# Attention over 513 tokens: 128-row score tiles with the 513th token apart, two heads at a time in TensorE's row halves, and every other product in one PSUM bank

## The reference, cut to what matters

```python
b, l, _ = x.shape                      # 4, 513, 192; H = 8, DK = 64, DV = 24, N_POS = 32
h1 = _rmsnorm(x, norm1_w)
q = (h1 @ wq).reshape(b, l, H, DK)
k = (h1 @ wk).reshape(b, l, H, DK)
v = (h1 @ wv).reshape(b, l, H, DV)
basis = _rel_basis(l, N_POS)           # (513, 513, 32), depends on j - i alone
qw = jnp.einsum('bihd,hdn->bihn', q, w_pos)
qr = jnp.einsum('bihn,ijn->bhij', qw, basis)
uk = jnp.einsum('hd,bjhd->bhj', u_param, k)[:, :, None, :]
vw = jnp.einsum('hd,hdn->hn', v_param, w_pos)
vr = jnp.einsum('hn,ijn->hij', vw, basis)[None]
bias = (qr + uk + vr) * scale
scores = jnp.einsum('bihd,bjhd->bhij', q, k) * scale + bias
attn = jax.nn.softmax(scores, axis=-1)
out = jnp.einsum('bhij,bjhd->bihd', attn, v)
out = out.reshape(b, l, H * DV) @ wo + bo
x = out + skip
```

## Time and profile before

| | us |
|---|---|
| median of 3 runs | 1121.22 (1118.86 to 1128.76) |
| the profiled execution | 1127.92, its span 1126.0 |
| PE busy | 956.4 (85%) |
| DVE busy | 724.2 (64%) |
| ACT busy | 671.5 (60%) |
| POOL busy | 134.1 (12%) |

### The profile page before, as it was taken

One profiled execution on the slowest core, in us unless ns is written; L12 is line 12 of the kernel. 1 busy time (PEld: TensorE's weight loads), 2 busy tenths in 40 slices (PEclk: granted clock), 3 DMA queues, 4 the chain that ended last, 5 costly groups with the idle time before them and its releaser, 6 DMA issues. The chain is left out here.

```text
span 1126.0 us, 20694 instructions
## 1 busy us (share of the span) xinstructions
PE 956.4 (85%) x6722; PEld 825.2 (73%) x6722; DVE 724.2 (64%) x1567; ACT 671.5 (60%) x1196; POOL 134.1 (12%) x199
## 2 busy tenths in 40 slices
PE   2999999999978989897889888957869970999993
PEld 2999999999956766676567657736836650999992
DVE  6999979799437853876497449735653353555543
ACT  4656847668248864986597568844322314557555
POOL 1000000000001440244034304430000000000000
PEclk9999999999988998999999899987979995999996
DMA  7011101399326842683367238721001212422101
GB/s 238 20 55 30 52 10 33 65 134 142 60 68 188 274 120 63 209 262 104 113 219 240 58 113 253 233 72 37 1 1 29 56 28 72 112 65 72 45 0 56
DMA packets 78721, 112.67 MB, mean 100 GB/s; under 512 B 10917, under 2 KB 38866, under 8 KB 78562
## 3 DMA queue, kind: packets, MB, share of 16 engines
q1 hardware_dynamic: 78658, 111.93, 37.7%
HBM read 61.07 MB, written 47.68 MB: 97 GB/s over the span
## 5 line engine op out<-in xcount | busy, mean ns | idle before, releaser
L405 PE MATMUL psum<-w,feat 128*128 128x192 f32 x960 | 166.0, 328 | 0.0
L405 PEld LDWEIGHTS psum<-w,feat 128*128 128x128 f32 x960 | 155.4, 191 | 0.0
L792 POOL TENSOR_SCALAR a_scores<-a_scores,a_inv 112x514 f32<-112x514 f32 (+1 forms) x160 | 112.6, 705 | 299.9 <-DVE a_inv L1138 299.9
L1123 DVE CUSTOM_DVE_ANT_0 a_scores<-psum,a_bias 112x514 f32<-112x514 f32 (+1 forms) x160 | 109.7, 688 | 49.6 <-PE psum L865 41.1
L422 PE MATMUL psum<-w_parts,parts 128*128 128x384 f32 x384 | 120.2, 378 | 24.4 <-DVE parts L228 21.5
L1015 ACT ACTIVATE a_scores<-a_scores,a_least 112x514 f32<-112x514 f32 (+1 forms) x160 | 116.6, 729 | 14.1 <-DVE a_least L1123 13.5
L878 PE MATMUL psum<-ident,a_scores 112*112 112x112 f32 (+1 forms) x800 | 103.4, 262 | 14.0 <-DVE a_probsT L1133 8.8
L328 ACT ACTIVATE feat<-turn 128x1024 f32<-128x1024 f32 (+1 forms) x60 | 58.4, 974 | 86.0 <-DVE turn L211 47.3
L865 PE MATMUL psum<-a_kh,a_q 128*112 128x258 f32 (+1 forms) x320 | 100.1, 334 | 7.1 <-DVE a_q L1093 4.2
L878 PEld LDWEIGHTS psum<-ident,a_scores 112*112 112x112 f32 (+1 forms) x800 | 78.5, 138 | 36.6 <-POOL a_scores L792 16.9
L819 PE MATMUL psum<-h1T,place 96*128 (+3 forms) x320 | 87.8, 413 | 13.3 <-DVEq L1086 6.9
(11 more groups left out here) (217 smaller groups left out, 1777.0 us busy)
## 6 DMA issues: line engine op xcount, KB each, us to landing
shear<-a_pos SPq DMA_DIRECT2D x128, 224.9 KB, 3.8
a_bias<-shear SPq DMA_DIRECT2D x128, 224.4 KB, 3.9
shear<-zero SPq DMA_DIRECT2D x20, 448.9 KB, 17.8
e_fc<-in_e_fc_dram SPq DMA_DIRECT2D x8, 672.0 KB, 5.8
x<-in_xT_dram SPq DMA_DIRECT2D x20, 256.0 KB, 2.8
e_proj<-in_e_proj_dram SPq DMA_DIRECT2D x8, 576.0 KB, 6.4
shear<-a_pos SPq DMA_DIRECT2D x32, 130.5 KB
a_bias<-shear SPq DMA_DIRECT2D x32, 130.3 KB
```

The source lines that it names most:

```text
L405: mm = pe.matmul(sums[m][:, 0:D], feat[:, r, j, 0, 128 * m:128 * m + 128], w[:, k, :], start=False, stop=ends)
L792: pool.tensor_scalar(row, row, inv[0:TILES[g % NT][1], g % TT:g % TT + 1], 1.0, ALU.mult, ALU.mult).then_inc(weighed, 1)
L1123: dve.tensor_tensor_reduce(halves(scores[0:r, g % TT, 0:PADL]), psum2(score_pair(g), r), halves(bias[0:r, g % MR, :]), -1.0 / 8, BIG, ALU. ...
```

## The change: what it does

- A score tile has 128 queries, so a head has four tiles and an image 32. Query 513 of all eight heads is computed apart (`score_row`, `row_position`, `row_values`, in 36 partitions), and key 513 is left out of the transposes: its probabilities come through a small matmul (`last_keys`) and one more matmul in `values`. Tiles go in the order head within a group of four heads, tile, group.
- Two heads are scored together (`score`). Head 2p lies in partitions 0 to 63 of `q` and `k`, head 2p+1 in 64 to 127. Per window of 258 keys there are three terms (hi hi, lo hi, hi lo), each as two matmuls of 64 rows, one for each head, into banks of their own. One call fills banks 0 to 3 and waits until both tiles of the pair before have been read.
- `put` moves a tile's four blocks in one copy, ACT the even tiles and DVE the odd ones, from bank 6. `position` uses banks 4 and 5.
- Everything else is one of 41 jobs an image, all in bank 7. A job waits for `job_out` of the one before. An image has 16 steps of two tiles, with one to three jobs in a step: step 0 keys and q; 1 values and q; 2 two projects and k; 3 two projects and keys; 4 v, v and keys; 5 v_last, values and k; 6 q, q, keys; 7 k, k, row_position; 8 p, p, keys and the extra row; 9 values and q; 10 q, k, keys and the row's transpose; 11 row_values and k; 12 q, q, keys; 13 values and p; 14 p, k, keys; 15 k. A q, k or p job is one window of 257 columns for one pair of heads or group.
- Products of the next image (`OF_NEXT`, 12 jobs) and the end of the image before (`OF_BEFORE`, 6 jobs) stand among the tiles, so an image has no part without tiles. Image 0 is written out, images 1 and 2 loop, image 3 is written out, and `finish` ends it. Twelve products (`START`) come first.
- `stack` for the next image is split: 12 DMAs after step 9 and 12 after step 15 on SP. The second copy of keys (L994, L1104) is gone. The 97-row input copy `load_image` moves from DVE to POOL.

The diff, cut to its core:

```diff
+    ROWS, NTILE, PAIRS = s.SROWS, N // s.SROWS, H1 // 2
+    NG, NU2 = H1 * NTILE, H1 * NTILE // 2
+    AHEAD, LAG = 8, 4
+    RT, MR, TT, RING = 4, 8, 8, s.RING
...
+    TERMS = (("hi", "hi"), ("lo", "hi"), ("hi", "lo"))
...
+    head_of = lambda g: G4 * (g // (G4 * NTILE)) + g % G4
...
+    pair_of = lambda u: 2 * (u // (2 * NTILE)) + u % 2
...
+    JOBS = [
+        ("keys", 1, 3), ("q", 2, 0),
...
+        ("p", 0, 0), ("p", 0, 1), ("keys", 0, 3),
...
+    JOBS_AT = [2, 2, 3, 3, 3, 3, 3, 3, 3, 2, 3, 2, 3, 2, 3, 1]
...
+    OF_BEFORE = [n for n, (kind, a, i) in enumerate(JOBS) if kind == "project" or (kind, a, i) in (("keys", 1, 3), ("values", 1, 1))]
+    OF_NEXT = [n for n, (kind, a, i) in enumerate(JOBS) if (kind in "qk" and a < 2) or kind == "p"]
...
+            def image(b, first, more):
+                for u in range(NU2):
+                    for g in (2 * u + AHEAD, 2 * u + AHEAD + 1):
+                        if g < NG:
+                            store(b, g, first)
+                        elif more:
+                            store(b + 1, g - NG, False)
+                        if g - LAG < NG:
+                            load(b, g - LAG, first)
+                        elif more:
+                            load(b + 1, g - LAG - NG, False)
+                    if more and u == 9:
+                        stack(b + 1, 0)
+                    if more and u == NU2 - 1:
+                        stack(b + 1, 1)
 
             stack(0, 0)
...
+            def last_keys(b, hg, t):
+                g = hg * (NG // 2) + G4 * t
+                pe.wait_ge(weighed, b * NG + g + G4)
+                stand_alone(pe, passed)
+                return pe.matmul(s.bank[JOB][32 * hg:32 * hg + G4, 0:ROWS],
+                                 scores[:, g % TT:g % TT + G4, L - 1:L].rearrange("p g n -> p (g n)"), s.ident[:, :],
+                                 start=True, stop=True)
...
+                for jb in range(NTILE):
+                    for n in range(G4):
+                        h = hg * G4 + n
+                        pe.matmul(s.bank[JOB][VW * n:VW * n + VW, 0:2 * ROWS], v[:, jb, VW * h:VW * h + VW],
+                                  probsT[:, n, jb, 2 * ROWS * w:2 * ROWS * (w + 1)], start=jb == 0, stop=False, skip_group_check=True)
+                return pe.matmul(s.bank[JOB][:, 0:2 * ROWS], v_last[:, 128 * hg:128 * hg + 128],
+                                 lastT[:, 2 * ROWS * w:2 * ROWS * (w + 1)], start=False, stop=True,
+                                 skip_group_check=True)
...
+            def job(b, n, first, more):
+
+                kind, a, i = JOBS[n]
+                pe.wait_ge(job_out, NS + NJ * b + n)
+                if (first and n in OF_BEFORE) or (not more and n in OF_NEXT):
+                    pe.sem_inc(job_out, 1)
...
+            def score(b, u, first):
+                p, i0 = pair_of(u), ROWS * tile_of(2 * u)
+                if u or not first:
+                    pe.wait_ge(biased, b * NG + 2 * u)
+                if u == 9:
...
-                    for w in range(2):
-                        for k in (kh, kl):
-                            mm = pe.matmul(pairs[score_pair(g)][w][0:r, 0:HALF + 1], q[:, h, i0:i0 + r],
-                                           k[:, h, w * HALF:w * HALF + HALF + 1], start=k is kh, stop=k is kl)
...
+                for w in range(2):
+                    for n, (q_part, k_part) in enumerate(TERMS):
+                        for e in range(2):
+                            rows = slice(DK1 * e, DK1 * e + DK1)
+                            mm = pe.matmul(s.bank[2 * e + w][:, 0:HALF + 1], q[q_part][rows, p, i0:i0 + ROWS],
+                                           k[k_part][rows, p, w * HALF:w * HALF + HALF + 1], start=n == 0, stop=n == 2)
+                            if w == 1 and n == 2:
+                                mm.then_inc(scores_done, 1)
...
+            def score_row(b):
+                pe.wait_ge(biased, b * NG + 2 * 8 + 1)
+                pe.wait_ge(row_q_set, b * 2 + 2)
+                pe.wait_ge(job_out, ended(b, "k", 3, 1))
+                stand_alone(pe, passed)
+                for w in range(2):
+                    for p in range(PAIRS):
+                        for n, (q_part, k_part) in enumerate(TERMS):
+                            mm = pe.matmul(s.bank[w][0:RW, 0:HALF + 1], row_q[:, p, ("hi", "lo").index(q_part), :],
+                                           k[k_part][:, p, w * HALF:w * HALF + HALF + 1], start=p == n == 0, stop=p == PAIRS - 1 and n == 2)
...
+            def flip(b, g, first):
+                pe.wait_ge(weighed, b * NG + g + 1)
+                if g % 2:
+                    pe.wait_ge(put_a, b * (NG // 2) + g // 2 + 1)
+                elif g or not first:
+                    pe.wait_ge(put_d, b * (NG // 2) + g // 2)
+                for jb in range(NTILE):
+                    mm = pe.transpose(s.bank[FLIP][:, ROWS * jb:ROWS * jb + ROWS], scores[:, g % TT, ROWS * jb:ROWS * jb + ROWS],
+                                      s.ident[:, :])
...
+
+                score(b, u, first)
+                job(b, jobs[0], first, more)
+                behind(2 * u - 2)
+                ahead(2 * u + AHEAD)
+                if len(jobs) > 1:
+                    job(b, jobs[1], first, more)
+                ahead(2 * u + AHEAD + 1)
+                behind(2 * u - 1)
+                if u == 8:
+                    score_row(b)
+                if u == 10:
+                    pe.wait_ge(put_d, b * (NG // 2) + 10)
+                    flip_row(b)
+                if len(jobs) > 2:
...
+                act.wait_ge(job_done, count)
+                if kind == "p":
+                    if not first:
+                        act.wait_ge(stacked[a], 16 * 3 * G4 * i)
+                    act.copy(parts[:, a, 0, window(w)], s.bank[bank][:, 0:HALF]).then_inc(hi_done, 1)
+                    if w:
+                        act.wait_ge(rest1, i * 4 + a * 2 + 2)
+                        act.copy(parts[:, a, 1, :], rest[:, :]).then_inc(part2, 1)
+                else:
+                    if not first:
+                        last = 2 * NTILE * (a // 2) + 2 * NTILE - 2 + a % 2
+                        act.wait_ge(scores_done, i * NG - NG + 2 * last + 2)
+                        act.wait_ge(row_scored, i)
+                    dst = (q if kind == "q" else k)["hi"]
+                    act.copy(dst[:, a, window(w)], s.bank[bank][:, 0:HALF]).then_inc(hi_done, 1)
...
+                jobs = list(range(first_job(u), first_job(u) + JOBS_AT[u]))
+                job(b, jobs[0], first, more)
+                weigh(b, 2 * u)
+                if 2 * u + AHEAD < NG:
+                    position_out(b, 2 * u + AHEAD, first)
+                elif more:
+                    position_out(b + 1, 2 * u + AHEAD - NG, False)
+                if u:
+                    put(b, 2 * u - 2, first)
+                elif not first:
+                    put(b - 1, NG - 2, False)
+                if len(jobs) > 1:
+                    job(b, jobs[1], first, more)
+                weigh(b, 2 * u + 1)
+                if u == 8:
+                    weigh_row(b)
+                if u == 10:
+                    put_row(b)
+                if len(jobs) > 2:
+                    job(b, jobs[2], first, more)
+
...
-                    dve.wait_ge(rest1, i * 2 + p + 1)
-                    dve.sem_inc(prod_free, 1)
+                    dve.tensor_tensor(rest[:, window(w)], s.bank[bank][:, 0:HALF], parts[:, a, 0, window(w)], ALU.subtract).then_inc(rest1, 1)
+                    dve.wait_ge(rest1, i * 4 + a * 2 + w + 1)
+                    dve.sem_inc(job_out, 1)
                 else:
...
+            def add_bias_row(b, first):
+                dve.wait_ge(row_scored, b + 1)
+                dve.wait_ge(job_out, ended(b, "row_position", 0, 0))
+                if not first:
+                    dve.wait_ge(job_done, ended(b - 1, "row_values", 0, 0))
+                stand_alone(dve, passed)
+                dve.tensor_tensor_reduce(halves(row_scores[:, :]), psum2(0, RW), halves(row_bias[:, :]), -1.0 / 8, BIG, ALU.add,
+                                         ALU.min, row_least[:, :]).then_inc(row_biased, 1)
...
+                add_bias(b, 2 * u, first)
+                add_bias(b, 2 * u + 1, first)
+                job(b, jobs[0], first, more)
+                invert(b, 2 * u)
+                if len(jobs) > 1:
+                    job(b, jobs[1], first, more)
+                if 2 * u + AHEAD + 1 < NG:
+                    position_out(b, 2 * u + AHEAD + 1, first)
+                elif more:
+                    position_out(b + 1, 2 * u + AHEAD + 1 - NG, False)
+                if u:
+                    put(b, 2 * u - 1, first)
+                elif not first:
+                    put(b - 1, NG - 1, False)
+                invert(b, 2 * u + 1)
+                if u == 8:
+                    add_bias_row(b, first)
```

(4 more changed lines are left out.)

834 lines of the change are left out of this document (423 added, 411 removed), and 9 rows, old and new, of the table JOBS.

## The result

Slower. The changed kernel takes 1152.63 us in the median (1151.0 to 1155.27), against 1121.78 for the kernel before on the same chip: ratio 1.0261, 95% interval 1.0218 to 1.0305. The forecast was 1111. The profiled execution has a span of 1149.2, against 1126.0 before; all of these 23.2 us lie in the attention.

A forecast was written before the change was run, and what follows sets the result against it. Before, PE was busy 88% of each image with some 20 us of waits; after, a chain of ACT's and DVE's lists around one bank. Start -11, images 0, tail +1 gave 1118 profiled, 1111 median; range 1078 to 1152.

The forecast's parts named there:

- the sum: Whole kernel: start -11, images 0, tail +1, giving -10 against the profiled execution, 1118.
- Start: Before the first bias addition: it comes at about 341 instead of 352.3, a gain of 11 us.
- The chain: Inside the images: ACT's list, then DVE's, in series around one bank; plain step 5.5 us, looped image 100.
- No engine is full: Plain step of 5.5 us: PE's own work is 4.35 and DVE's 3.9, so no engine fills it.
- covered, with about 1 us to spare: SP after steps 9 and 15: loads behind 7.6 us of stack DMAs, issued 12 to 13 us ahead, arrive in time.
- Biases come late: Rival, chance 0.08: slower stack or loads behind it cost up to 5 us at six places; +30, 1141.
- PE waits for a DVE put: Step 10, before the 513th query's transpose: this wait is part of a step priced at 6.9 us.
- 34 one-column matmuls: Step 11, for the 513th query: they take 3 us (bounds 1 and 5) of a 7.1 us step.
- Tail: After the last addition: 14.5 us against 13.5, four projects through one bank; a loss of 1.
- Shape changes: Rival, chance 0.14: array shape changes cost PE up to 0.17 us, two in each of 64 steps; +22, 1133.
- the last two rivals: Row halves not running at once, chance 0.13, +42, 1153; biases coming late, chance 0.08, +30, 1141.
- The forecast of no gain in the images: Four images: 384 us against 383.7 before; product stages vanish and their work returns as longer steps.

The follow-up runs named there:

- e7_mute: Loads of stack spread, plus ScalarE's and VectorE's copies of sixteen query and key products an image dropped, against e1_spread; 1134.3 us, ratio 1.0086.
- e8_lighter: Against e1_spread, fewer TensorE matmuls for the value rows (4 for 8 a job) and the 513th query's scores (8 for 24); 1133.38 us.
- e6_one_half: Against e1_spread, both heads of a pair take queries and keys from rows 0 to 63; 1203.37 us, ratio 1.0662.
- e3_fill: Against the changed kernel, TensorE also runs unread products in the last image; 1145.24 us, ratio 1.0174.
- e9_flip_later: Against e5_best, the 513th query's flip moved behind step 11's scores and its values to step 11's second product; 1126.48 us, ratio 0.9992.
- e12_loads: Against e11_both, the four load groups for the next image's first half issued one place earlier each; 1119.43 us, ratio 0.9941.
- e11_both: Against e5_best, the edits of e9_flip_later plus the 513th query's scores made in the middle of step 8; 1122.88 us, ratio 0.9978.
- e2_serial: Against the changed kernel, three score matmuls of head 0 put ahead of head 1's, not alternating; 1153.87 us, ratio 1.0247.
- e4_noprod: Against the changed kernel, query and key products among the tiles left out, the first image's reused; 1148.94 us, ratio 1.0175.
- e5_best: Against the changed kernel: loads spread, last image filled, last four projections each in a bank of its own; 1136.38 us, ratio 1.0095.
- e1_spread: Against the changed kernel, each head's three stack DMAs issued at a step of their own; 1145.23 us, ratio 1.0165.

## Why the prediction was wrong

Against the profiled execution before, the sum said 10 us less and the profile has 23.2 more. The 33 us between them lie in the four images, 4.0, 6.9, 8.1 and 9.9, and in the tail, 3.6.

**Start: right.** The first bias addition stands at 341.2, forecast 341.

**The chain: right in kind.** The plain step is 5.5, step 8 is 9.1 (forecast 9.2), and the copies of the products are on the chain of the thin steps (e7_mute). But "No engine is full" holds of the plain step alone. In step 4 TensorE's own work sets the length (e8_lighter), where the forecast had it by way of ACT's exponential, and step 8 goes in part with TensorE's work. For steps 1, 5, 9 and 13 it is argued, not shown: with the loads spread, PE is busy for 96 to 100% of them in the third image. That every step grew in e6_one_half does not tell the two apart, since the scores stand in front of the addition in either account.

**The step that failed first: "covered, with about 1 us to spare".** The lead of the bias loads was taken as two steps of 12 to 13 us. Behind the second `stack` lie steps 15 and 0, the shortest, 10.4 us together; 7.75 go to the issues, and after them each store must land (2.9 us in the median) before its load can go (3.6 more). Cost 3.8, 3.3 and 4.1 us in three images, 11 of the 33. A part of that is TensorE's wait of 2.3 to 3.1 us for VectorE in step 2, and its clock behind it. The rival "Biases come late" had the mechanism, chance 0.08 and price 30, at six places; the first `stack`, behind step 9, cost no late bias.

**The step that failed next: no term for the clock.** The sum priced every matmul at the full level; the clock stands in the forecast's range only, although already had images of 0.92 to 0.98. In the changed kernel slots fall to the lower level for several us in step 11 of every image (0.77, 0.63, 0.52 and 0.50), in the last image, in the tail. The last image was forecast 88 and took 97.9: 4 us of biases, and 5 more returned when TensorE was filled (e3_fill). The flip that the forecast priced in step 10 ("PE waits for a DVE put") was worth 3.7 us or more a place in e9_flip_later, not the wait alone. How much of the 33 us the clock made in all stays open. The kernel of e12_loads ran its third image at a clock of 1.00 in 98.6 us, where the forecast had 100 for the order before these edits.

**Luck in step 11.** The forecast gave step 11 7.1 us, and the second image has 7.1. But its 34 one-column matmuls, twice, were priced 3 us and take 1.4 at the full level (614.58 to 615.93 in e9_flip_later, the step 5.5): too dear a price stood in for the clock that was missing, and the miss would have been larger without it.

**Tail:** 18.1 for 14.5. The four projections were priced near 1.6 each and took 1.68; what was missed is their clock of 0.81 and the work in front of them.

**Shape changes:** from the first score to the job behind it the forecast took 0.8; the rows have 0.9 to 1.0 (451.76 to 452.67, 586.51 to 587.51). That is 0.1 to 0.2 a step. It can be a part of steps 4 and 13 at 6.9 and 7.0 for 6.5, but step 9, of the same kind, has its 6.5. By the Trainium skill, "TensorEngine Tiling (Array Packing)", Key Properties, a change of tiling mode drains TensorE; the trace agrees with a small price. No run here took it away by itself, so what it makes of an image stays open. So does why single slow stretches fall where they do: steps 15 and 0 had one in some kernels and none in others with the same rows. The forecast had also read its row on shapes twice: 386.11 to 386.43 gave 0.25 for a position tile in the prices and 0.15 in the rival (the tile takes 0.23, 584.88 to 585.11).

**The chances:** half of the shape case and the last two rivals are 0.28, where 0.25 was written. That moves nothing.

The forecast of no gain in the images missed by 29 of the 33 us: they took 412.9 for 383.7 before. What it had right is that the product stages held TensorE's work, which came back among the tiles.

## What to carry to other kernels

Before merging a stage into a loop, count what the fullest engine gets: here ACT lost a third of its work, TensorE none, and the kernel became slower. A short wait on TensorE can cost more than its length; look at the granted clock behind it, and move the waiter behind work that is ready. One transpose moved by a step, with the row's values behind a product, gave 10 us. Put a block of DMA issues of several us in pieces between the stores and loads it shares a queue with, above all ahead of short steps; and look at who waits for the last piece, which came up to 2.3 us late in e11_both.

## What the runs showed of the hardware

- TensorE ran matmuls of two row halves in pairs though three of one half stood ahead of three of the other in the program (e2_serial: slots of 0.12 as before, the starts of a pair 10 ns apart). The Trainium skill, "TensorE: Matmul & The Clock Gate", Part 3, has matmuls start and end in program order; these records do not agree.
- Two halves at once cost 0.12 us a pair of 258 columns, one half twice 0.24 (e6_one_half): a factor of two, nothing lost inside the group. The first slot of the group is longer by 0.1, with one half as with two.
- Work taken from TensorE can cost as much as it gives: sixteen products an image less left the images as long, at a mean clock of 0.874 for 0.923 (e4_noprod, the slowest of its four runs).
- A wait of 1.42 us was followed by 6.8 us at the lower level (e5_best, 620.0 to 626.8), in an image in which TensorE was busy 91% of the time. At this place, ahead of the 513th query's transpose, waits of 1.4 to 1.5 us were followed by the lower level in each of the first three images of four kernels (the changed one, e1_spread, e3_fill, e5_best).
- The length of a wait alone does not decide it: in step 2, waits of 3.09 us (changed kernel, 564.44) and of 2.82 and 2.77 (e3_fill) were followed by no lower level, and one of 2.25 (changed kernel, 456.69) was.
